# Search counts and their all-ones weights as rounded floats, with a tensor of their own for the counts

## What is computed

```python
# first layer, per batch: a 0/1 mask of the 10240 largest entries of a product
att = softmax(x, axis=-1) / sqrt(1024)
adj = emb_s * emb_t * att            # diagonal set to -inf
_, idx = top_k(adj.reshape(g, n * n), 10240)
x = x + mask_of(idx)                 # 1.0 at the chosen places
# second layer: attention with 16 heads of 64
xn = rms_norm(x, g_norm) * (1 + scale) + shift      # scale, shift = cond @ W_emb + b_emb
q, k, v = split(xn @ W_qkv)
q, k = rms_norm(q, g_q), rms_norm(k, g_k)
o = softmax(q @ k.T / 8) @ v
x = x + o + o @ W_out
```

## Time and profile before

| | us |
|---|---|
| median of three runs | 3567.34 |
| lowest and highest | 3564.81, 3569.01 |
| profiled execution | 3572.17 |
| span of its instructions | 3570.4 |

### The profile page before, as it was taken

The page is one execution under the profiler, slowest core; times in us unless marked ns, Lnnn a source line. Parts: engine busy times, 40 slices in busy tenths (PEclk is TensorE's granted clock), DMA queues, the critical chain, the costliest instruction groups (busy, mean ns, idle before and its releaser), DMA issues.

```text
span 3570.4 us, 47811 instructions
## 1 busy us (share of the span) xinstructions
PE 3419.1 (96%) x17164; PEld 2605.1 (73%) x17175; DVE 2441.1 (68%) x3757; ACT 2054.8 (58%) x3374; POOL 2494.5 (70%) x2600
## 2 busy tenths in 40 slices
PE   4978999999999999999999999999999999999999
PEld 2446888888646788888756788888855788888867
DVE  8975778887885788877887688887787333333332
ACT  4765666666735565665646365666654466666670
POOL 2038888888747777777747677777756578888870
PEclk9997999999999999999999999999999999999999
DMA  8033333333354222222255222222225332222223
GB/s 319 1 121 127 107 112 107 111 108 107 126 176 161 98 89 89 89 89 89 77 176 190 101 89 89 96 103 103 90 102 182 112 142 98 104 98 104 98 88 104
DMA packets 165757, 407.97 MB, mean 114 GB/s; under 512 B 12120, under 2 KB 83856, under 8 KB 155536
## 3 DMA queue, kind: packets, MB, share of 16 engines
q1 hardware_dynamic: 165520, 404.91, 31.8%
HBM read 306.29 MB, written 98.57 MB: 113 GB/s over the span
## 4 chain that ended last, share of the span: by engine, by line
PE 79%; DVE 7%; POOL 6%; ACT 4%; issue 2%; DMA 1%; SPq 0%; POOLq 0%; DVEq 0%; ACTq 0%
PE pax L1794 28%; PE pst L1851 12%; PE ppv L1873 11%; PE pax L1831 7%; PE ppv L1880 6%; PE pst L1747 5%; PE pst L1766 3%; PE pst L1539 2%; PE pax L1812 2%; POOL xlo L640 2%; DVE trash L1181 2%; DVE xr L1231 1%; ACT pf L1034 1%; POOL pl L616 1%; PE ppv L1890 1%
## 5 line engine op out<-in xcount | busy, mean ns | idle before, releaser
L616 POOL TENSOR_TENSOR pl<-pf,ph 128x1024 fp32r<-128x1024 f32 x512 | 1221.5, 2397 | 168.5 <-ACT pf L1034 167.7
L1181 DVE TENSOR_SCALAR_CACHE_REDUCE trash<-keys,state 128x2048 uint8<-128x2048 f32 x384 | 900.0, 2344 | 9.9
L1456 DVE TENSOR_REDUCE mx<-pax 128x1 f32<-128x512 f32 x960 | 657.8, 691 | 183.0 <-PE pax L1831 174.9
L1028 ACT ACTIVATE ph<-pst 128x1024 fp32r<-128x1024 f32 x512 | 523.2, 1022 | 250.8 <-PE pst L1851 200.2
L1034 ACT ACTIVATE pf<-pst 128x1024 f32<-128x1024 f32 x512 | 522.2, 1020 | 0.3 <-DMA out_x<-pf 0.3
L1442 DVE TENSOR_REDUCE ss<-sq 128x4 f32<-128x260 f32 x256 | 108.3, 423 | 603.2 <-ACT sq L994 580.5
L1831 PE MATMUL pax<-sA 65*128 65x512 f32 x960 | 394.1, 416 | 23.0 <-ACT sA L1014 20.7
L714 POOL TENSOR_TENSOR rs<-ss,half 128x4 f32<-128x4 f32 x256 | 263.7, 1030 | 203.1 <-DVE ss L1442 203.1
L1794 PE MATMUL pax<-wh,xh 128*128 128x384 f32 x1912 | 387.0, 345 | 4.8 <-DVE mx L1456 4.7
L1794 PE MATMUL pax<-wl,xh 128*128 128x384 f32 x1912 | 389.7, 341 | 0.0
L1794 PEld LDWEIGHTS pax<-wh,xh 128*128 128x128 f32 x1912 | 341.7, 191 | 30.6 <-DVE mx L1456 6.6
(11 more groups left out here) (266 smaller groups left out, 5687.5 us busy)
## 6 DMA issues: line engine op xcount, KB each, us to landing
xl<-xl_scr SPq DMA_DIRECT2D x224, 512.0 KB, 3.2
wh<-w_scr SPq DMA_DIRECT2D x24, 1536.0 KB, 6.3
wl<-w_scr SPq DMA_DIRECT2D x24, 1536.0 KB, 9.6
keys<-in_x SPq DMA_DIRECT2D x32, 512.0 KB, 4.9
xl_scr<-xlo SPq DMA_DIRECT2D x64, 256.0 KB, 3.4
pf<-out_x SPq DMA_DIRECT2D x64, 256.0 KB, 3.8
out_x<-pf SPq DMA_DIRECT2D x64, 256.0 KB, 3.1
oT_scr<-ostg SPq DMA_DIRECT2D x56, 256.0 KB, 2.0
```

What stands on the lines that cost most here:

```text
L616: e.tensor_tensor(pl[:, w % 3, :], pf[:, w % 3, :], ph[:, w % 3, :].bitcast(F32), ALU.subtract).then_inc(t_lo, 1)
L1028: e.activation(ph[:, w % 3, :], src, ACT.Exp, scale=DH ** -0.5).then_inc(t_eh, 1)
L1181: e.tensor_scalar(trash[:], kv, thr_f, None, ALU.is_ge, ALU.add, accum_out=cnt[:, c:c + 1]).then_inc(z_cnt, 1)
L1456: e.tensor_reduce(mx2[:, j // T, j % T, c:c + 1], max_banks(alone, j)[:, c, :], axis=AX, op=ALU.max).then_inc(m_mx, 1)
```

## The change

The matrix of ones becomes a float32r tensor `allpr`; `allp` is now a float32 view of the same words, which `search_alone`, `before` and `rows_below` go on using. A new float32r tensor `beside`, 128x4, takes the counts of the search beside the pairs, and `search_sum` multiplies `allpr` and `beside`, both float32r. `pre`, `r0` and `rank` become three columns of one tensor. In the built program the order of the instructions on every engine is the same; only these operands differ. The tensors between `mz` and `reach` begin 32 bytes later, and those from `rank` on, the large tensors for features, weights and scores among them, 32 bytes earlier. `keys`, `wh`, `stage`, `qkn` and `trash` stay where they are.

```diff
--- before.py
+++ after.py
@@ -89,7 +89,9 @@
     gain_qk = sb("gain_qk", [P, DH])
     identr = sb("identr", [P, P], F32R)
     ident = identr[:].bitcast(F32)
-    allp = sb("allp", [P, P])
+    allpr = sb("allpr", [P, P], F32R)
+    allp = allpr[:].bitcast(F32)
+    beside = sb("beside", [P, 4], F32R)
     mz = sb("mz", [P, 2, DH + T], F32R)
     mx2 = sb("mx2", [P, 2, T, 2])
     paramsT = sb("paramsT", [P, NC + 24])
@@ -97,11 +99,12 @@
     s_sb = sb("s_sb", [P, B, T])
     small = {n: sb(n, [P, w]) for n, w in dict(
         ss=8, rs=8, half4=4, rl=T, kmx=T, knm=T, kz=T, krz=T, kw=T, cnt=8, tot4=4, tot=1, neq=1, reach=1,
-        pre=1, r0=1, rank=1, carry=1, ssx=T, rsx=T).items()}
+        rank=3, carry=1, ssx=T, rsx=T).items()}
     ss, rs, half4, rl = (small[n] for n in ("ss", "rs", "half4", "rl"))
     kmx, knm, kz, krz, kw = (small[n] for n in ("kmx", "knm", "kz", "krz", "kw"))
-    cnt, tot4, tot, neq, reach, pre, r0, rank, carry, ssx, rsx = (
-        small[n] for n in ("cnt", "tot4", "tot", "neq", "reach", "pre", "r0", "rank", "carry", "ssx", "rsx"))
+    cnt, tot4, tot, neq, reach, carry, ssx, rsx = (
+        small[n] for n in ("cnt", "tot4", "tot", "neq", "reach", "carry", "ssx", "rsx"))
+    pre, r0, rank = (small["rank"][:, n:n + 1] for n in range(3))
     state = sb("state", [P, 3], I32)
     prefix, cand, thr = state[:, 0:1], state[:, 1:2], state[:, 2:3]
     bit, acc = (sb(n, [P, 1], I32) for n in ("bit", "acc"))
@@ -585,7 +588,7 @@
             e.affine_select(out=tri(0), in_=tri(0), compare_op=ALU.is_gt, fill=0.0, base=0,
                             pattern=[[1, P]], channel_multiplier=-1).then_inc(c_pool, 1)
             e.memset(ones, 2.0).then_inc(c_pool, 1)
-            e.memset(allp[:], 1.0).then_inc(c_pool, 1)
+            e.memset(allp, 1.0).then_inc(c_pool, 1)
             e.memset(vh[:].bitcast(F32).rearrange("p a t h d -> p (a t h) d")[:, :, DH:DH + 1], 1.0).then_inc(c_one, 1)
             e.memset(vl[:].bitcast(F32).rearrange("p a t h d -> p (a t h) d")[:, :, DH:DH + 1], 0.0).then_inc(c_one, 1)
             e.sem_inc(t_lo, CST)
@@ -1179,7 +1182,7 @@
             kv = keys[:].rearrange("p t n -> p (t n)")[:, c * CHUNK:(c + 1) * CHUNK]
             e.wait_ge(z_cnt, CST + 4 * z + c)
             e.tensor_scalar(trash[:], kv, thr_f, None, ALU.is_ge, ALU.add,
-                            accum_out=cnt[:, c:c + 1]).then_inc(z_cnt, 1)
+                            accum_out=beside[:, c:c + 1]).then_inc(z_cnt, 1)
 
         def search_update(self, z):
 
@@ -1278,16 +1281,16 @@
             e, n = self.e, F_STEPS * b
             e.wait_ge(f_tri, b + 1)
             e.tensor_reduce(neq[:], ppv[:, 0, 4:8], axis=AX, op=ALU.add).then_inc(f_dve, 1)
-            e.tensor_reduce(pre[:], ppv[:, 0, 0:4], axis=AX, op=ALU.add).then_inc(f_dve, 1)
+            e.tensor_reduce(pre, ppv[:, 0, 0:4], axis=AX, op=ALU.add).then_inc(f_dve, 1)
             e.wait_ge(f_dve, n + 6)
             ties = neq
             if b == 0:
                 e.copy_predicated(carry[:], acc[:], neq[:]).then_inc(y_up, 1)
                 e.wait_ge(y_up, 7 * STEPS + 12)
                 ties = carry
-            e.scalar_tensor_tensor(r0[:], pre[:], ties[:], reach[:], ALU.subtract, ALU.add).then_inc(f_dve, 1)
+            e.scalar_tensor_tensor(r0, pre, ties[:], reach[:], ALU.subtract, ALU.add).then_inc(f_dve, 1)
             e.wait_ge(f_dve, n + 7)
-            e.tensor_scalar(rank[:], r0[:], -1.0, float(TOPK), ALU.mult, ALU.add).then_inc(f_dve, 1)
+            e.tensor_scalar(rank, r0, -1.0, float(TOPK), ALU.mult, ALU.add).then_inc(f_dve, 1)
             e.wait_ge(f_dve, n + 8)
 
         def boundary(self, ob, fb, kb):
@@ -1398,7 +1401,7 @@
 
             e, equal = self.e, first_equal[:, t * N:(t + 1) * N]
             e.wait_ge(f_step, 3 * t + 3)
-            e.scalar_tensor_tensor(equal, first_rank[:], rank[:], equal, ALU.is_le, ALU.mult).then_inc(f_dve, 4)
+            e.scalar_tensor_tensor(equal, first_rank[:], rank, equal, ALU.is_le, ALU.mult).then_inc(f_dve, 4)
 
         def finalise_tile(self, b, t):
             e, n, r = self.e, F_STEPS * b + 8 + 4 * t, side(b)
@@ -1411,7 +1414,7 @@
             e.wait_ge(f_dve, n + 2)
             e.tensor_tensor_scan(scn[r][:], eqm[r][:], eqm[r][:], carry[:], ALU.add, ALU.max).then_inc(f_dve, 1)
             e.wait_ge(f_dve, n + 3)
-            e.scalar_tensor_tensor(eqm[r][:], scn[r][:], rank[:], eqm[r][:], ALU.is_le, ALU.mult).then_inc(f_dve, 1)
+            e.scalar_tensor_tensor(eqm[r][:], scn[r][:], rank, eqm[r][:], ALU.is_le, ALU.mult).then_inc(f_dve, 1)
             if t < 6:
                 e.wait_ge(d_xin[t % 2], 16 * (3 * b + t // 2 - 1))
             else:
@@ -1540,7 +1543,7 @@
                                  stop=(alone and j == cuts[-1] // WIDE - 1), skip_group_check=True)
                 if not alone:
                     e.wait_ge(y_act, z)
-                    i = e.matmul(pst[:, 0, 0:1], allp[:], cnt[:, 0:1], start=False, stop=True, skip_group_check=True)
+                    i = e.matmul(pst[:, 0, 0:1], allp, cnt[:, 0:1], start=False, stop=True, skip_group_check=True)
                 i.then_inc(y_sum, 1)
                 if z == STEPS // 2:
                     e.wait_ge(d_wemb, 16)
@@ -1662,7 +1665,7 @@
                 e.wait_ge(f_dve, F_STEPS * b + 4)
             wait(e, c_tri, 2 * b)
             e.matmul(ppv[:, 0, 0:4], tri(b), cnt[:, 4:8], start=True, stop=True)
-            e.matmul(ppv[:, 0, 4:8], allp[:], cnt[:, 4:8], start=True, stop=True).then_inc(f_tri, 1)
+            e.matmul(ppv[:, 0, 4:8], allp, cnt[:, 4:8], start=True, stop=True).then_inc(f_tri, 1)
 
         def features(self, b, g, ob, q):
 
@@ -1801,7 +1804,7 @@
         def search_sum(self, z, bank=0):
             e = self.e
             e.wait_ge(z_cnt, CST + 4 * z + 4)
-            e.matmul(pax[:, bank, 6 * DH:6 * DH + 4], allp[:], cnt[:, 0:4], start=True, stop=True).then_inc(z_sum, 1)
+            e.matmul(pax[:, bank, 6 * DH:6 * DH + 4], allpr[:], beside[:], start=True, stop=True).then_inc(z_sum, 1)
 
         def transpose_tile(self, gp, t):
             e, u = self.e, T * gp + t
```

## The result

| | median, us | lowest to highest | runs |
|---|---|---|---|
| before | 3567.34 | 3559.2 to 3569.01 | 5 |
| after | 3546.47 | 3542.49 to 3550.46 | 5 |

The profiled execution took 3542.49 us (span 3540.8 us, mean granted clock 0.990), against 3572.17 us, 3570.4 us and 0.985 before.

A forecast was written before the change was run, and what follows sets the result against it. TensorE was taken to bound the kernel; one load less at each of 96 sums, 8.9 us in pairs 0 to 6 plus 1.7 us late, gave 10.6 us: 3567.34 - 10.6 = 3556.8 us, range 3551 to 3563.5 us.

The forecast's parts named there:

- What bounds the kernel: Whole kernel: TensorE, matmuls busy 96% of the span and 79% of the chain; time spared there should come off the end.
- the removed loads: Search sums beside the pairs: 96 second weight loads and 96 second matmuls go from TensorE, 96 x 0.11 = 10.6 us.
- The choice of 0.11 over 0.08 us: Gain per sum: 0.11 us from load spacing at a pair's start; 0.08 us, from whole pairs, as lower bound.
- The price of 0.19 us for the whole sum: Tile 4 of a pair: 2.43 us with a sum, 2.24 us without, so the whole float32 sum costs 0.19 us.
- The 15 late sums: Sums of pair 7 and the boundary: each gains a load like the others, 15 x 0.11 = 1.7 us.
- The 32-byte moves at nothing: Tensors beginning 32 bytes earlier or later: taken to cost nothing, slower operand reads being left to a rival.
- Given back to GpSimd and VectorE: Searching pairs: TensorE, ahead, waits for GpSimd's low part of `values`; gain partly lost, 3560.9 to 3563 us; chance 0.15.
- More than one load: Each sum: the remaining rounded load gets cheaper too, 15.4 to 18 us gained, 3552.0 us at 15.4; chance 0.06.
- Nothing changes: The sums: TensorE still gets two passes for the narrow product, 3567.3 us; chance 0.05.
- Slower: Large tensors 32 bytes earlier: TensorE reads them slower; 1.9 ns per product cancels the gain, 3.5 ns gives 3576.8 us; chance 0.05.

## Why the prediction was wrong

**What bounds the kernel, and the removed loads: right.** 96 loads and matmuls went, bare at 0.11 us each. The kernel that has this part alone took 3556.4 us against the 3556.8 us forecast, at an equal clock 9.4 us less than before for the 10.6 us of the sum, and doubling the sums gives 11.3 us back. The choice of 0.11 over 0.08 us is borne out by 0.44 us for four sums in whole pairs without a move. The price of 0.19 us for the whole sum was right too: a rounded sum still costs 2.29 - 2.20 = 0.09 us at tile 4.

**The 15 late sums: counted too high.** The prediction had them gain a load each, 0.55 us for the five of pair 7 and the boundary of one batch, because "nothing stands between that could hide 0.11 us". It read this from the second sum and took it over to the others. Of ScalarE and TensorE behind the first sum, before:

```profile
2610.24 1.02 ACT L1034 ACTIVATE pf<-pst 128x1024 f32<-128x1024 f32 x1
2611.14 0.18 ACT L985 ACTIVATE tot<-pax 128x4 f32<-128x4 f32 x1
```

After, with both sums:

```profile
2585.36 1.02 ACT L1037 ACTIVATE pf<-pst 128x1024 f32<-128x1024 f32 x1
2585.88 0.17 PE L1807 MATMUL pax<-beside,allpr 128*128 128x4 f32 x1
2586.26 0.18 ACT L988 ACTIVATE tot<-pax 128x4 f32<-128x4 f32 x1
2597.79 0.27 PE L1807 MATMUL pax<-beside,allpr 128*128 128x4 f32 x1 [1.40 <-DVE trash L1184]
2598.10 0.17 ACT L988 ACTIVATE tot<-pax 128x4 f32<-128x4 f32 x1 [1.12 <-PE pax L1807]
```

Behind the second sum the addition comes 0.31 us after it instead of 0.42 us, a load earlier. Behind the first it comes 0.38 us after it where it came 0.39 us, since ScalarE is at its copy until then, and from the first sum to the second are 11.91 us (before 11.93 us): nothing was gained there. In pairs 7 without a fall of the clock, the update behind the boundary's sum starts 52.7 us behind the pair's start in the changed kernel and 53.0 us before, 0.3 us less instead of 0.55 us. So the 15 sums are worth some 0.9 us and not 1.7 us, and 8.9 + 0.9 = 9.8 us stands closer to the 9.4 us measured at an equal clock. Doubling just these 15 costs 3548.9 - 3547.9 = 1.0 us at an equal clock, which agrees.

**The 32-byte moves at nothing: the step that failed.** They are worth 7.5 us. The prediction had the mechanism among its rivals, but with one sign only. Its evidence was that `wh`, on a multiple of 64, and `wl`, 32 behind one, give products of 345 and 341 ns. Those two are the moving operands. The stationary one of both groups is `xh`, 32 behind a multiple of 64 in both, so the rows said nothing of what its move does; and alone it is worth 3.9 of the 7.5 us, while all the others without it gain nothing. Part of the 4 ns between these means was the clock: in the pairs of before, without the stretches at the lower level, they are 340.7 and 338.0 ns. With a price unknown in size and sign, the range should have gone as far down as it went up: the rival had 1.9 to 3.5 ns for each product as a loss, and the products with `xl` gained 3.2 ns each (5.8 us over 1792).

**The clock: left out.** The profile of before had a pair 0 some 2 us longer than its neighbours in batches 1 to 3, and a pair 7 of 42.4 us at a clock of 0.96 beside one of 40.8 us at 1.00. The prediction worked from a sum of durations at full clock and never asked whether sparing a load would change when TensorE falls to its lower level. In pair 7 it does.

**The rivals.** "Given back to GpSimd and VectorE": did not happen. The wait for VectorE's counts in pair 7 stayed at 14.9 us in all, as the earlier trace rows had it (that figure counts the waits of the weight load and of its matmul, 8.9 and 6.0 us), and no new wait for `pl` came in pairs 1 to 6 of the searching batches: each has one wait of TensorE, 0.5 us for ScalarE, as before. "More than one load", with the fast weight load of the Trainium skill ("TensorE: Matmul & The Clock Gate", Weight-path perf modes): not so; the rounded loads take 188 ns like the float32 ones, and two of them start 0.11 us apart. "Nothing changes": fell by the counts. "Slower": the right place with the wrong sign.

**The chances.** The sign and the class, faster by more than 0.2% at 0.75, were right. The range missed by 4.5 us, less than the move's 7.5 us alone.

## What to carry to other kernels

A sum over partitions by a matrix of ones costs its weight loads, not its columns: rounded operands take one load where float32 takes two. Where TensorE set the pace, the load that was spared came off whole (0.44 us for four in a pair); in the serial chain of pair 7 and the boundary only 0.3 of 0.55 us did, for another engine's work stood behind the first sum. Follow such a chain at each of its steps and not at one. A change that adds or joins a small tensor moves everything allocated behind it. Read the addresses before and after, and give such a move a price with both signs, or test it alone by a pad of the same size. Before giving a gain of 0.3% to an edit, compare the granted clock stretch by stretch, since one stretch at the lower level is worth as much as 15 to 30 of these loads.

## What the runs showed of the hardware

The place of operands in memory changes the pace of TensorE: with `xh` on a multiple of 64 bytes and all behind it too, products of 384 columns with `xl` have a mean of 335 ns instead of 339 ns, and a pair takes 0.2 us less in 86. It is not a matter of one tensor alone, and 64 bytes earlier is not as before: 350.0 us for the group instead of 352.1 us, yet pairs 0.1 us longer. And 96 bytes earlier, on a multiple of 64 too, is worth 4.8 us and not 7.5 us at an equal clock.

The fall of the granted clock depends on small things: with one more bare load, 0.11 us, and its matmul at each sum of pair 7 there were 14 falls in 24, without it none in 18. The same kernel, at the start of a batch, shows it in one profile and not in the next. What sets it there stays open.
